# The first layer's experts by slots: 71 gathered tiles, twelve to a self job, in place of all eight experts for every row

## The reference

```python
x = x + tanh(g_xattn[0]) * cross_attention(ctx, layernorm(x), b, lens)          # "copy" jobs, u = 0
# u = 1, the "self" jobs: attention and a dense mixture of experts on the same normed rows
n = layernorm(x)
attn = self_attention(n @ W_qkv + b_qkv)
gate = softmax(n @ W_gate + b_gate)                  # [16, 256, 8]
top_g, top_i = top_k(gate, 2)
combine = sum(one_hot(top_i, 8) * top_g[..., None], axis=2)
expert_out = einsum('bsd,edf->bsef', n, W_experts) + b_experts
x = x + tanh(g_ffn[0]) * (attn + einsum('bsef,bse->bsf', expert_out, combine))
x = x + tanh(g_xattn[1]) * joint_attention(layernorm(x), ctx) @ w_proj.T + ...   # "joint" jobs, u = 2
x = x + tanh(g_ffn[1]) * layernorm(h + moe2(h)), h = layernorm(z + causal_attention(z)), z = layernorm(x)   # u = 3, then expert phase
```

## Time and profile before

| | us |
|---|---|
| median of 3 runs | 2596.88 (2596.45 to 2602.02) |
| the profiled execution: its own time | 2595.37 |
| the profiled execution: span | 2593.6 |
| first to last `FIN` of the copy jobs | 96.3 to 360.6 |
| last `FIN` of the self jobs | 975.1 |
| TensorE busy over the span | 2280.5 (88%) |
| VectorE, ScalarE, GpSimd busy | 1658.5, 1358.8, 1004.2 |

### The profile page before, as it was taken

How to read it: one execution, slowest core, us unless ns; L and a number is a source line. 1 busy time by engine, 2 the same in 40 slices (tenths; PEclk the granted TensorE clock), 3 DMA queues, 4 the chain that set the end, 5 groups by cost and what they waited for, 6 DMA issues and landing times. The chain is left out here.

```text
span 2593.6 us, 51898 instructions
## 1 busy us (share of the span) xinstructions
PE 2280.5 (88%) x17492; PEld 1577.5 (61%) x17493; DVE 1658.5 (64%) x4377; ACT 1358.8 (52%) x2398; POOL 1004.2 (39%) x1875
## 2 busy tenths in 40 slices
PE   2889999899999999999999999999837999999950
PEld 1444555555455556666666666766527999999950
DVE  4878886677766667777767777786644434343437
ACT  3889863555336456777777788776601222222212
POOL 5556412213022135333323347887611333333323
PEclk9999998999999999999999999999956999999985
DMA  7878623314134245555555445555264111111125
GB/s 219 208 187 205 159 72 82 76 46 114 44 90 96 64 98 134 123 119 121 127 129 123 119 103 123 137 125 131 54 217 147 34 36 34 36 35 34 36 84 194
DMA packets 212014, 279.68 MB, mean 108 GB/s; under 512 B 32734, under 2 KB 156617, under 8 KB 205546
## 3 DMA queue, kind: packets, MB, share of 16 engines
q1 hardware_dynamic: 198378, 246.57, 38.5%
q0 software_dynamic: 6912, 17.97, 2.2%
q10 hardware_dynamic: 6528, 12.58, 1.3%
HBM read 193.12 MB, written 84.83 MB: 107 GB/s over the span
## 5 line engine op out<-in xcount | busy, mean ns | idle before, releaser
L1012 ACT ACTIVATE ex<-t_ps 128x512 f32<-128x512 f32 (+1 forms) x1280 | 684.9, 579 | 200.8 <-PE t_ps L918 153.8
L1163 DVE TENSOR_REDUCE mx<-s_ps 128x2 f32<-128x512 f32 (+1 forms) x1024 | 660.0, 683 | 198.4 <-PE s_ps L889 123.8
L918 PE MATMUL t_ps<-qs,ks 123*128 123x256 bf16 x2048 | 354.8, 276 | 9.6 <-ACT ex L1012 4.6
L941 PE MATMUL pv_ps<-ex,va 128*17 128x256 f32 (+1 forms) x5120 | 318.3, 375 | 0.7 <-POOL ex L1064 0.5
L1006 ACT ACTIVATE qs<-tr_ps 27x2048 bf16<-27x2048 bf16 x128 | 239.2, 1869 | 107.8 <-PE tr_ps L902 104.9
L918 PEld LDWEIGHTS t_ps<-qs,ks 123*128 123x128 bf16 x2048 | 176.4, 98 | 156.2 <-ACT ex L1012 68.3
L1571 PEld LDWEIGHTS x_up_ps<-x_rows_t,x_wnow 128*128 128x128 f32 x2272 | 267.3, 193 | 5.3 <-issue 0.9
L859 PE MATMUL pre_ps<-wexp,xt 128*128 128x512 f32 x512 | 266.3, 625 | 3.7 <-DVE moe L1225 2.7
L1571 PE MATMUL x_up_ps<-x_rows_t,x_wnow 128*128 128x128 f32 x2272 | 267.9, 277 | 1.1 <-ACT x_rows_t L1601 1.1
L1601 ACT ACTIVATE x_rows_t<-x_rt_ps 128x256 f32<-128x256 f32 x72 | 27.6, 383 | 448.5 <-PE x_rt_ps L1560 448.5
L1581 PE MATMUL x_y_ps<-wdn,x_act 128*128 x1136 | 257.1, 379 | 0.7 <-DVE x_y L1642 0.7
(11 more groups left out here) (244 smaller groups left out, 3741.4 us busy)
## 6 DMA issues: line engine op xcount, KB each, us to landing
q_parts<-pq SPq DMA_DIRECT2D x128, 192.0 KB
qs<-q_parts SPq DMA_DIRECT2D x64, 384.0 KB, 4.9
qs<-q_parts SPq DMA_DIRECT2D x192, 128.0 KB, 5.8
k_parts<-pk SPq DMA_DIRECT2D x96, 192.0 KB
ks<-k_parts SPq DMA_DIRECT2D x96, 192.0 KB
ks<-k_parts SPq DMA_DIRECT2D x288, 64.0 KB
ks<-ctx_k_parts SPq DMA_DIRECT2D x64, 192.0 KB
ks<-ctx_k_parts SPq DMA_DIRECT2D x192, 64.0 KB
```

What stands on the lines that cost most here:

```text
L918: last = pe.matmul(dst[:, t * T:(t + 1) * T], key[0:ROWS, h, t * P:(t + 1) * P], qs[q_at][0:ROWS, h, :], start=True, stop=True)
L941: last = pe.matmul(pv_ps[i * VS:i * VS + VW, q0:T], val[:, t, k * QH + i, :], e, start=r == 0 and t == 0, stop=r == srcs - 1 and t == NT - ...
L1012: act.activation(ex[:, n % EXPS, 0:w], t_ps[n % 2][:, 0:w], ACT.Exp).then_inc(t_read, 1)
L1163: dve.tensor_reduce(dst, s_ps[n % S_BANKS][:, :].rearrange("p (a b) -> p a b", a=dst.shape[-1]), AX.X, ALU.max).then_inc(s_read, 1)
```

## The change

The first layer's dense experts go. After each copy job the norm of the next kind is made at once (`HNS`, `HNP`, `HNX`, into the job's `o` buffer), stored (`STOREN`), turned (`HT`) and multiplied with the gate weights (`HG`); a self job loads those rows (`LOADN`) instead of making them. When all 16 batches' logits are there, a chain on VectorE (`RC` 0 to 22, with `RX` on ACT, `RANK` and 16 `NAME` chunks on PE, `RH` and `TH` on DVE and POOL) makes the three tables of `route()` for the first layer. It belongs to job (1, 0). Then 71 tiles, twelve each to jobs (1, 2) to (1, 7): `XR` gathers 128 rows, `XTT` turns them (two transposes, copy by ACT), `XE` adds bias and product with the one expert whose number PE has read from the table (`value_load`), DVE copies, `XS` scatters. A joint job loads both result rows of each of its rows (`LOADY`) and adds them to x (`MOE`) ahead of its norm. `w1` and `wo` of the causal jobs now lie in the experts' place and are loaded with `LOADX` of job (3, 0) rather than at the start; the start makes some more constants (five iotas and masks, the biases in three bf16 parts). The core of the diff:

```diff
-    "GATE": [("pe", 0.9), ("dve", 0.65)], "GEXP": [("act", 0.22)], "TOP": [("dve", 0.6)],
-    "CT": [("pe", 0.25), ("act", 0.36)], "MBIAS": [("pe", 1.1), ("dve", 0.69)], "EXPERT": [("pe", 0.87), ("pe", 0.87), ("dve", 0.97)],
+    "STOREN": [("sp", 0.5), ("wire", 6.0)], "LOADN": [("sp", 0.5), ("wire", 5.0)], "LOADY": [("sp", 0.5), ("wire", 6.5)], "MOE": [("dve", 1.95)],
+    "RC": [("dve", 0.95)], "RX": [("act", 0.42)], "RANK": [("pe", 0.9), ("dve", 0.72)],
+    "RH": [("dve", 0.67)], "TH": [("dve", 0.45), ("pool", 0.8)], "NAME": [("pe", 0.9), ("dve", 0.25)],
+    "XR": [("pool", 1.25), ("wire", 4.5)], "XTT": [("pe", 0.55), ("act", 0.39)], "XE": [("pe", 1.0), ("dve", 0.42)], "XS": [("pool", 1.25), ("wire", 4.5)],
...
+HOTS = 4
+CHUNKS = TOPK * TILES // HOTS
+NER, NY = 6, 4
+CHAIN = 23
+
+
+def tile_job(n):
+    return 1, 2 + n // 12
...
+        c = add("LOADC", 0, ("RC", 1, 0, CHAIN - 1) if u == 2 and b < NCTX else None, ("VC", *before, 0) if before else None, ("KT", *before, 0) if before and before[0] == 0 else None)
...
-    s = add("LNS", 0, x, past("LNX", 2))
-    s = add("LNX", 0, add("LNP", 0, s), past("XT", 2) if u < 3 else None)
-    free = [past(n, NQ, 0, (1, 2, 3)) for n in ("K", "Q", "V")] + [past("EXPERT", NQ, (t, e), (1,)) for t in range(NT) for e in range(0, E, 2)]
+    if u == 1:
+        s = add("LOADN", 0, ("STOREN", 0, b, 0), past("XT", 2))
+    else:
+        if u == 2:
+            y = add("LOADY", 0, *([("MOE", u, b - 2, 0)] if b >= 2 else [("XS", *tile_job(n), n) for n in range(SLOT_TILES)]))
+            x = add("MOE", 0, x, y)
+        s = add("LNS", 0, x, past("LNX", 2, 0, (0, 2, 3)))
+        s = add("LNX", 0, add("LNP", 0, s), past("XT", 2) if u < 3 else None)
+    free = [past(n, NQ, 0, (1, 2, 3)) for n in ("K", "Q", "V")] + [past("HG", NQ, 0, (0,))]
...
-        add("FIN", 0, *outs, *(experts if u == 1 else []))
+        s = add("FIN", 0, *outs)
...
+    if u in (0, 3):
+        s = add("HNX", 0, add("HNP", 0, add("HNS", 0, s, ("HNX", u, b - 2, 0) if b >= 2 else None)))
+        if u == 0:
+            add("STOREN", 0, s)
+            s = add("HT", 0, s, past("HG", NQ))
+        else:
+            s = add("HT", 0, add("HNG", 0, s), ("HG", u, b - 2, 0) if b >= 2 else None)
         add("HG", 0, s)
...
+    add(rc(0), *[("HG", 0, b, 0) for b in range(B)])
+    add(("RX", 1, 0, 0), rc(0))
+    for k in range(1, CHAIN):
+        after = {1: ("RX", 1, 0, 0), 9: ("RANK", 1, 0, 0), CHAIN - 2: ("NAME", 1, 0, CHUNKS - 1)}.get(k)
+        add(rc(k), rc(k - 1), after)
+    add(("RANK", 1, 0, 0), rc(7))
+    for k in range(CHUNKS):
+        ready = rc(18 + 2 * (k // (CHUNKS // TOPK)))
+        free = ("NAME", 1, 0, k - 2) if k >= 2 else None
+        add(("NAME", 1, 0, k), add(("RH", 1, 0, k), ready, free), add(("TH", 1, 0, k), ready, free), ("NAME", 1, 0, k - 1) if k else None)
+
+    def of(name, n):
+        return (name, *tile_job(n), n) if n >= 0 else None
+
+    for n in range(SLOT_TILES):
+        add(of("XR", n), rc(CHAIN - 1), of("XTT", n - NER))
+        add(of("XTT", n), of("XR", n), of("XE", n - 2))
+        add(of("XE", n), of("XTT", n), of("XS", n - NY))
+        add(of("XS", n), of("XE", n))
...
+                    elif name == "XTT":
+                        if k == 0:
+                            pe.wait_ge(tables_ready, 1)
+                        chosen[k] = pe.value_load(expert_of[0:1, k:k + 1], min_val=0, max_val=E - 1)
+                        begin_pre(step)
+                        pe.wait_ge(er_loaded[k % NER], 16 * (k // NER + 1))
+                        for c in range(DC):
+                            last = pe.transpose(bank[:, c * P:(c + 1) * P], er[k % NER][:, c * P:(c + 1) * P], ident[:, :])
...
+                    elif name == "XE":
+                        wait_copied(pe, ("XTT", u, b, k))
+                        x = chosen.pop(k)
+                        pe.matmul(bank[:, 0:D], tile_is[:, k:k + 1].broadcast_to([3 * E, P]), bexp_parts[:, :], start=True, stop=False)
+                        for c in range(DC):
+                            last = pe.matmul(bank[:, 0:D], ert[k % 2][:, c, :], wexp[:, c, bass.ds(x, 1), :].rearrange("p e n -> p (e n)"),
+                                             start=False, stop=c == DC - 1)
...
+                    elif name == "XR":
+                        if k == 0:
+                            pool.wait_ge(tables_ready, 1)
+                            for m in range(B):
+                                nth, at = rows_stored(m)
+                                pool.wait_ge(n_stored[at], 16 * nth)
+                        if k >= NER:
+                            wait_turned(pool, ("XTT", *tile_job(k - NER), k - NER))
+                        pool.indirect_dma_start(er[k % NER], None, n1_d.rearrange("b p t n -> (b p t) n"),
+                                                bass.IndirectOffsetOnAxis(ap=row_of[:, k:k + 1].bitcast(U32), axis=0)).then_inc(er_loaded[k % NER], 16)
+                    elif name == "XS":
+                        wait_copied(pool, ("XE", u, b, k))
+                        pool.indirect_dma_start(y1_d.rearrange("b p t n -> (b p t) n"), bass.IndirectOffsetOnAxis(ap=dest_of[:, k:k + 1], axis=0),
+                                                ey[k % NY], None, bounds_check=ROWS_OUT - 1, oob_is_err=False).then_inc(y_stored[k % NY], 16)
...
+                    elif name == "XE":
+                        if k >= NY:
+                            dve.wait_ge(y_stored[k % NY], 16 * (k // NY))
+                        end_pre(step, dve.tensor_copy(ey[k % NY], bank[:, 0:D]))
+                    elif name == "MOE":
                         dve.wait_ge(x_loaded[x_at], 16 * (nth_x + 1))
+                        dve.wait_ge(y_loaded[b % 2], 16 * (b // 2 + 1))
+                        for m in range(TOPK):
+                            for t in range(NT):
+                                last = dve.scalar_tensor_tensor(out=xs[x_at][:, t, :], in0=yb[b % 2][:, t * TOPK + m, :], scalar=first_share[:, b * NT + t, m:m + 1],
+                                                                in1=xs[x_at][:, t, :], op0=ALU.mult, op1=ALU.add)
...
+                        if u == 2:
+                            s.wait(s.n)
+                            dve.wait_ge(moe_added, MOE_AT[("MOE", u, b, 0)] + 1)
...
-                    elif name == "GATE":
-                        logits = bank[:, 0:NT * E].rearrange("p (t e) -> p t e", t=NT)
-                        end_pre(step, dve.tensor_tensor(lg[r][:, :, :], logits, bg0[:, :].unsqueeze(1).broadcast_to([P, NT, E]), ALU.add))
...
-                    elif name == "EXPERT":
-                        t, e = k
-                        wait_copied(dve, at_of[("moe", b, t)])
-                        for n in range(2):
-                            if n:
-                                s.wait()
-                            last = dve.scalar_tensor_tensor(out=moe[r][:, t, :], in0=bank[:, n * D:(n + 1) * D], scalar=comb[r][:, t, e + n:e + n + 1],
-                                                            in1=moe[r][:, t, :], op0=ALU.mult, op1=ALU.add)
...
+                        if step == ("LOADX", 3, 0, 0):
+                            sp.dma_start(w1, chunked(a["w1_qkv"])).then_inc(norm_loaded, 16)
+                            sp.dma_start(wo, chunked(a["w1_o"])).then_inc(norm_loaded, 16)
+                            sp.dma_start(g1, a["ln1_g"].partition_broadcast(P)).then_inc(norm_loaded, 16)
...
```

More of the change, by code:

```diff
@@ L195, in job_steps @@
         bp = add("BPROJ", 0, s)
-    if u == 1:
-        chain = add("GEXP", 0, add("GATE", 0, turned, ("FIN", u, b - 2, 0) if b >= 2 else None))
-        for n in range(TOPS):
-            chain = add("TOP", n, chain)
-        chain = add("MBIAS", 0, add("CT", 0, chain))
-        experts = [add("EXPERT", (t, e), chain) for t in range(NT) for e in range(0, E, 2)]
     outs = []
@@ L328, in rank @@
 def rank(op):
-    return 0 if op[0][0] in ("OT", "FIN", "M", "MT") else 1
+    return 0 if op[0][0] in ("OT", "FIN", "M", "MT", "RC", "RX", "RANK", "RH", "TH", "NAME") else 1
 ORDER, BEGUN, DONE = orders()
@@ L395, in wait_stored, with rows_stored @@
     eng.wait_ge(stored[JOB[job] % NX], 16 * (JOB[job] // NX + 1))
+def rows_stored(b):
+    at = JOB[(0, b)] % NO
+    return sum(JOBS[j][0] == 0 for j in range(at, JOB[(0, b)] + 1, NO)), at
 def joint_stored(u, b):
@@ L814, in _ @@
                 had = collections.Counter()
+                chosen = {}
                 for step in ORDER["pe"]:
@@ L1098, in _ @@
                     j = JOB[(u, b)]
-                    r = b % 2 if u == 1 and name not in ("LNS", "LNX") else j % 2
+                    r = j % 2
                     nth_x, x_at = uses_before("x", (u, b))
```

411 lines of the change are left out of this document (295 added, 116 removed).

## The result

The changed kernel takes 2613.93 us (median of 7 runs, 2609.67 to 2617.46) where the kernel before takes 2599.36 beside it: a ratio of 1.0054, 95% interval 1.0043 to 1.0066. It is slower by 14.6 us; forecast were 2500, and a gain. The profiled execution has a span of 2611.2 us, 17.6 over the one before.

What follows compares the result with a forecast made beforehand. TensorE was taken to bound the self jobs, GpSimd the tiled ones after the change. Self jobs -119.5, copy jobs +18, joint jobs +4, start +1 gave -96.5 us, hence 2500 us; the 8-in-10 range was 2450 to 2590.

Steps and rivals of the forecast that it cites:

- What goes: Self jobs: removing dense experts, bias product and gate frees 225 us of TensorE in 14 jobs, leaving 22 us a job.
- What a tile costs: Self jobs with tiles: 1.36 us of TensorE a tile; twelve tiles make a job 38.7 us there, 40.7 on GpSimd.
- the factor 0.85: Scaling of TensorE's group times, which overlap at their ends: groups add to 613.7 us while it is busy 522.
- GpSimd's part: Tiled self jobs: 24 transfers at 1.25 us plus 9.4 make 40.7 us a job; six jobs 244 us.
- The register read: TensorE's read of each tile's expert number: at most 0.75 us each, 53 us for 71, taken as nothing.
- The chain: Routing tables during self jobs 0 and 1: 75 us for both jobs, bounds 61 and 105.
- 0.968 of the time: The most an engine gets of a stretch, taken from TensorE's 96.8% in the joint jobs.
- The copy jobs: Added norm, HT, HG and store: pace 18.7 us, 1.1 more a job, 18 us in 16 jobs; bounds 10 and 42.
- Joint jobs: MOE's four operations of 0.48 us on VectorE and the longer way to XT: 4 us in all, bounds 0 and 31.
- The start: Some 21 small VectorE operations, about 6 us, before a wait for ScalarE: 1 us, bounds 0 and 6.
- the first (GpSimd hidden): Rival for the self jobs: transfers cost 1.0 to 1.1 us, TensorE alone rules; 2456 us, chance 0.2.
- The slower one: Rival: the 0.92 us before each transfer is GpSimd time, 1.91 to 2.15 us a transfer; 2600 to 2635 us, chance 0.1.

Runs made afterwards that it cites:

- e3: Changed kernel with plain transfers at fixed addresses instead of the indirect gathers and scatters: 2579.2 us, ratio 0.9928 to before.
- e5: e3 plus a 0.61 us GpSimd copy in front of each of the 142 transfers: 2576.8 us, ratio 0.9917.
- e1: Changed kernel without the choice of expert: tile k takes expert k modulo 8, TensorE reads no register; 2610.5 us, ratio 1.0052.
- e18: e11 with e1's edit, no choice of expert and no register read: 2566.2 us, ratio 0.9878.
- e4: Changed kernel without most of HT and HG in the copy jobs: 2599.9 us, ratio 0.9997.
- e8: e4 and also without most of the copy jobs' second norm, on 16 columns instead of 256: 2610.2 us, ratio 1.0038.
- e16: Changed kernel, whole computation, with HT of a copy job planned not before the next job's FIN: 2544.3 us, ratio 0.9803.
- e12: e8 with the bare norm, HT and HG steps also planned at 0.05 us or less: 2581.6 us, ratio 0.9944.
- e11: e9 with MOE planned at 0.05 us and the expert bias loads issued ahead of the weights: 2573.5 us, ratio 0.9904.
- e9: Changed kernel with six tiles a self job instead of twelve and a GpSimd copy before each indirect transfer: 2583.9 us, ratio 0.9948.
- e10: Changed kernel, whole computation, with MOE and the copy jobs' second norm steps planned at 0.05 us: 2676.2 us, ratio 1.0293.
- e15: e11 with the copy jobs' store of the norm issued from ScalarE's queue instead of SP's: 2573.7 us, ratio 0.9901.
- e13: Changed kernel with the copy jobs' store of the norm issued from ScalarE's queue instead of SP's: 2617.3 us, ratio 1.0061.
- e14: Changed kernel storing one partition's 2 KB of the norm instead of 256 KB: 2609.5 us, ratio 1.0039.
- e17: e11 with HT planned after the next job's FIN, as in e16: 2586.8 us, ratio 0.9965.
- e2: Changed kernel without most of MOE's adding, its four operations on 1 column instead of 256: 2592.8 us, ratio 0.9977.

## Why the prediction was wrong

The forecast was 2500; on the profiled execution it missed by 114.1 us. Step by step:

- *What goes* was right. TensorE's busy time without the tiles' products is 168.0 us in jobs 2 to 8 and 128.2 in 9 to 15 (e3), together 296.2, where 14 times the forecast's 21.2 are 296.8. But 19.6 us of it run before FIN of job 8, since later jobs run ahead; so jobs 9 to 15 take 19.5 us each, 17 less than 7 times 22, and the stretch with tiles is longer by as much.
- *What a tile costs*, TensorE's part, was nearly right: 1.48 us for 1.36, which is 8.6 us in all, and the factor 0.85 holds for the tiles' short steps too (0.84). Of the 37.5 us by which e3's 303.5 exceed the 266 forecast, 19.6 are the work that moved, 8.6 the tiles' price, and 9.3 more idle time of TensorE than the forecast left (30.3 for 21.0).
- *What a tile costs*, GpSimd's part, is the step that failed, and the largest term: it priced an indirect transfer by the time that it holds GpSimd alone. That time was right (1.25 forecast, 1.28 measured, gap included) and costs nothing: e5 puts it back and nothing moves. What the transfers do to the other engines stood at nothing, without a reason. It is 40.8 us in jobs 2 to 8 (344.3 less 303.5; 30 to 43 by the kernels on the same chips as e3 and e5). In 21.6 of them TensorE is busy for longer with the same 1756 products, at a clock of 0.90 for 0.96, and 19.2 are more idle time.
- The register read at nothing was right (e1, e18).
- *The chain*: 75 forecast, 93.5 measured, within its bounds. VectorE's work is 78.42 us for 69.5 forecast. Of the 8.9 more, 6.1 are RH and TH, at 0.77 and 0.61 us an operation for 0.61 and 0.38: at half the width they took more than half the time. And I let VectorE fill 0.968 of the time, and it fills 84%: NAME goes to TensorE and back 16 times, and VectorE stands 6.9 us for it in front of the sums alone.

```profile
L1396 DVE TENSOR_TENSOR work<-row_at,lane_f 128x512 f32<-128x512 f32 x16 | 12.3, 769 | 0.0
...
L1396 DVE TENSOR_TENSOR work<-tile_at,tile_f 128x292 f32<-128x292 f32 x16 | 9.7, 605 | 0.0
...
L1402 DVE TENSOR_TENSOR ctx<-pre_ps,ctx 128x73 f32<-128x73 f32 x15 | 3.5, 231 | 6.9 <-PE pre_ps L1006 6.7
```

- *The copy jobs*: +31.6 for +18, within the bounds of 10 and 42, in part with the wrong cause. I took a sum of engine times. Some 10 to 16 us are HT's and HG's time (e4), and the norm's time is none of it (e8). The rest goes with the order: e16 takes 22 us off by giving the tail time, but 12 of them come back in the chain. That the tail's way from engine to engine is the reason fits e12's waits and isn't shown by itself.
- *Joint jobs*: +22.7 for +4, within 31. 10.7 us are MOE's time, at 0.92 us an operation for 0.48; the other 12 go with the order laid around it. e11 has all of them back with MOE done in full: 8 with six tiles a job and room between the transfers, 15.5 more with MOE planned at nothing.
- *The start*: +8.5 for +1, outside its bounds of 0 and 6. I saw the steps but not that small_loaded now counts loads that stand behind w0 and wexp in SP's queue. The first FIN is at 101.5 to 105.3 us in the kernels with them there, and at 95.9 to 97.0 in those with them moved ahead.

Of the rivals, the first (GpSimd hidden) had the mechanism nearest to the truth and the time farthest. The slower one has the right side by a mechanism that isn't there: its gap of 0.92 us is 0.30. Its 0.1 was no insight. The range failed because the failed terms all leaned one way: each was a sum of engines' own times. The late signals, the hand-overs, the orders laid around new steps and the load that stands behind others are in no such sum.

What stays open: why TensorE's signals come late beside indirect transfers. With room between the transfers such waits went, on three chips on which kernels without room had them: e9 beside e10 (96.0 us) on one, e11 beside e12 (66.5) on the second, e15 beside e13 and e14 (55.3 and 45.1) on the third. So I took strings of transfers for the cause; but e16 has the longest strings and no such wait. e16, e17 and e18 ran on one chip, and there the trace holds all of TensorE's 513 signals of the two pre banks (e17 all but 2). Elsewhere e9, e11 and e15 lack 28 to 31 of them although spaced, the changed kernel, whose chip is not on record, lacks 22, and e3 and e5, with plain transfers, lack none where e1, e2 and e4 lack 18 to 29. So for e16 it may be the chip as well as its order. No other run without spacing is on record for that chip, so e16's 50 us in the self jobs, and with them its ratio, are not all shown to be the edit's.
